# Grouped attention: probabilities as fp16 halves turned by the DMA engines, where TensorE turned them in fp32

## The chip, the cores and the metric

One core of a Trainium2 chip runs the whole program. The metric is the time of one execution on the device in microseconds; the figure quoted is the median of several executions. The profile is of one such execution.

## What is computed

Two transformer layers over x of 4 batches x 256 tokens x 256 features, in this order: layer norm and an attention over a cache of 1601 keys plus 256 new ones; layer norm and a mixture of 32 experts; layer norm and the grouped cross attention that the change is about; layer norm and a ternary-weight network. Each result is added to x. The grouped attention is this:

```python
q = (hidden_states @ Wq).reshape(B, S, N_HEADS, HEAD_DIM)                # 4, 256, 16, 128
k = (encoder_hidden_states @ Wk).reshape(B, S_enc, N_KV_HEADS, HEAD_DIM) # 4, 1601, 4, 128
v = (encoder_hidden_states @ Wv).reshape(B, S_enc, N_KV_HEADS, HEAD_DIM)
q = rms_norm(q, q_norm_w)
k = rms_norm(k, k_norm_w)
k = jnp.repeat(k, groups, axis=2)                                        # groups = 4
v = jnp.repeat(v, groups, axis=2)
scores = jnp.einsum('bqhd,bkhd->bhqk', q, k) * scale
probs = jax.nn.softmax(scores, axis=-1)
out = jnp.einsum('bhqk,bkhd->bqhd', probs, v)
out = out.reshape(B, S, N_HEADS * HEAD_DIM)
return out @ Wo
```

## The kernel before

The program is written as four stages by hand, each with one instruction stream per engine and semaphores between them: `cached_attention`, `experts`, `grouped_attention` and `bit_ffn`. Products keep nearly fp32 accuracy by splitting each operand in two: HI is the value rounded to the format of the multiplier (fp32r), LO the remainder, and `product` issues three matmuls, HI x HI, HI x LO and LO x HI (`PARTS`).

`grouped_attention` works in **groups**: one batch with one of the four key-and-value heads, 16 groups in all. A group has eight **steps**, one for each of its four query heads and each half of 128 tokens; N = 128 steps, and `DRAIN` = 4 more at the end. Two steps make a **unit**: one head of 256 tokens. In step n:

- PE computes the scores of 128 tokens against 1601 keys into four PSUM banks `ps_s`, twelve matmuls (line 2021).
- DVE takes the maximum over the keys in `largest` (lines 1987, 1989) and announces it negated (line 1992).
- ACT takes the exponentials into `probs` in two pieces, 1200 and 401 keys, with their sums (`exp`, line 1844).
- For an earlier unit, PE turns the probabilities in 13 tiles of 128x128 (line 2070) into the ring of three PSUM banks `ps_t`; ACT copies HI out of it (line 1836) and DVE makes LO (line 1971) into `pT`. These are the jobs "pT".
- PE weighs the values of the unit before that: `weigh`, 39 matmuls in two halves, into `ps_m`. ACT takes the result out (`take_values`, line 1852).
- The sums' inverses (`invert`, DVE lines 1998 and 2001) go once per unit as a row through DRAM and back to all partitions (`invert_rows`, SP); POOL multiplies the result with them (line 1735), ACT makes HI (line 1859) and POOL makes LO (line 1738) of `oT`.

Beside this, each step has small jobs for the next group, dealt out by the table in `prepared`: the queries (`q`), keys and values (`kv`, 7 jobs of two key tiles, DVE lines 1958, 1959, 1961), their normalisation (`q_eps`, `k_eps`; POOL lines 1715, 1719, 1725, 1728), their transposes (`qT`, `kT`, DVE line 1967), the weights' splits (`split_q`, `split_kv`, `split_out` on ACT and POOL), and the output projection of the group before (`y`). At a batch's start there are also `norm`, `xT` and the encoder's splits (`enc`). All of PE, ACT and DVE go through the same list `plan[n]` in order, and all ring jobs share the three banks in order: a job waits until the job three places before it has been emptied by DVE.

The values `v` and `pT` are fp32r pairs. In `experts`, beside the products of the experts, the first group's keys and values are prepared.

## Time and profile before

| | |
|---|---|
| median of 3 executions | 1645.3 us (1642.59 to 1646.03) |
| the profiled execution, its own time | 1644.8 us |
| its span, first to last instruction | 1642.7 us |
| mean granted TensorE clock | 0.955 |
| first attention, to the start of the routing | about 180 us |
| routing and experts | about 180 to 423 us |
| grouped attention, prologue | about 423 to 458 us |
| grouped attention, 128 steps and drain | 458 to 1569 us |
| ternary network | 1569 to 1643 us |
| DMA traffic | 128 MB, 83691 packets |

Times in the trace are microseconds from the span's first instruction. A busy engine is not yet the bound: what matters in a stage is for whom the others wait. PE stands for the matmuls and PEld for the loads of their stationary operand, which overlap; DVE is VectorE, ACT ScalarE, POOL GpSimd, and SP the queue that issues the DMAs.

### The profile page before, as it was taken

What the parts mean: (1) busy time and instruction counts of PE and PEld (TensorE: products, weight loads), DVE (VectorE), ACT (ScalarE), POOL (GpSimd) and SP (SyncE); (2) the same over time, 40 slices, a digit from 0 to 9 for tenths busy, and PEclk for the clock granted to TensorE, in tenths of its full rate; (3) what the DMA queues carried; (4) which work ended last, traced back from release to release, by engine and by line L of the source; (5) the groups of instructions that cost most, each with busy time, mean ns of one, the idle gap of its engine ahead of it and who ended that gap; (6) DMA issues with size and microseconds to landing.
All of it is one profiled execution on the core that took longest, in us unless ns stands there. A gap on an engine that the chain in (4) does not pass through costs nothing. (4 is left out here: it accounts for less than half of the span.)

```text
span 1642.7 us, 27599 instructions
## 1 busy us (share of the span) xinstructions
PE 1443.0 (88%) x10080; PEld 1347.7 (82%) x10080; DVE 1161.6 (71%) x2372; ACT 982.1 (60%) x2065; POOL 570.5 (35%) x477
## 2 busy tenths in 40 slices
PE   6998378887679899999999899999989999999945
PEld 5888268776569898899999899999989999999823
DVE  4765688887567776667777667776766777677657
ACT  4564177887356565665656566566656656656536
POOL 3342154443355232342323343332234323322135
PEclk9999589999799999999999999999999999999968
DMA  6241479998223020101102011010101101001010
GB/s 202 77 168 58 153 246 295 299 299 282 61 46 78 20 70 10 50 20 27 43 8 70 20 40 42 8 43 16 59 20 39 43 8 43 21 7 27 23 52 26
DMA packets 83691, 128.05 MB, mean 78 GB/s; under 512 B 17284, under 2 KB 63496, under 8 KB 83176
## 3 DMA queue, kind: packets, MB, share of 16 engines
q1 hardware_dynamic: 79000, 113.84, 21.8%
q0 software_dynamic: 4560, 12.46, 3.1%
q8 instruction: 83, 1.36, 0.4%
q14 instruction: 48, 0.39, 0.1%
HBM read 114.28 MB, written 11.99 MB: 77 GB/s over the span
## 5 line engine op out<-in xcount | busy, mean ns | idle before, releaser
L1836 ACT ACTIVATE ga_pT<-ga_ps_t 128x512 fp32r<-128x512 f32 (+1 forms) x512 | 243.9, 516 | 256.5 <-PE ga_ps_t L2070 255.7
L1971 DVE TENSOR_TENSOR ga_pT<-ga_ps_t,ga_pT 128x512 fp32r<-128x512 f32 (+1 forms) x512 | 280.3, 583 | 94.3 <-ACT ga_pT L1836 92.3
L1844 ACT ACTIVATE ga_probs<-ga_ps_s,ga_neg_max 128x1200 f32<-128x1200 f32 (+1 forms) x256 | 235.7, 927 | 90.0 <-DVE ga_neg_max L1992 89.7
L2070 PE MATMUL ga_ps_t<-all_eye,ga_probs 128*128 128x128 f32 (+1 forms) x1664 | 227.0, 274 | 9.7 <-DVE ga_pT L1971 9.6
L2070 PEld LDWEIGHTS ga_ps_t<-all_eye,ga_probs 128*128 128x128 f32 (+1 forms) x1664 | 192.8, 141 | 19.7 <-DVE ga_pT L1971 12.6
L1987 DVE TENSOR_REDUCE ga_part_max<-ga_ps_s 128x1 f32<-128x1200 f32 x128 | 178.8, 1397 | 12.0 <-PE ga_ps_s L2021 10.5
L1738 POOL TENSOR_TENSOR ga_oT<-ga_out_n,ga_oT 128x256 fp32r<-128x256 f32 x64 | 47.6, 744 | 394.9 <-ACT ga_oT L1859 394.9
L2021 PE MATMUL ga_ps_t<-side_w_kv,side_encT 128*128 128x256 f32 (+1 forms) x1170 | 164.4, 290 | 13.9 <-DVE ga_pT L1971 8.6
L2021 PE MATMUL ga_ps_m<-ga_pT,ga_v 128*128 128x256 f32 (+1 forms) x1248 | 174.0, 286 | 2.6 <-DVE ga_pT L1971 2.4
L2021 PE MATMUL ga_ps_m<-ga_pT,side_v 128*128 128x256 f32 (+1 forms) x1248 | 174.6, 287 | 0.6 <-DVE ga_pT L1971 0.5
L2021 PEld LDWEIGHTS ga_ps_t<-side_w_kv,side_encT 128*128 128x128 f32 (+1 forms) x1170 | 147.0, 188 | 23.5 <-DVE ga_pT L1971 11.4
L2021 PE MATMUL ga_ps_s<-side_kT,ga_qT 128*128 128x400 f32 (+1 forms) x768 | 157.5, 354 | 6.1 <-ACT ga_probs L1844 6.0
L2021 PEld LDWEIGHTS ga_ps_m<-ga_pT,ga_v 128*128 128x128 f32 (+1 forms) x1248 | 157.1, 189 | 5.8 <-DVE ga_pT L1971 4.3
L2021 PEld LDWEIGHTS ga_ps_m<-ga_pT,side_v 128*128 128x128 f32 (+1 forms) x1248 | 157.8, 190 | 2.8 <-DVE ga_pT L1971 1.4
L2021 PE MATMUL ga_ps_s<-ga_kT,ga_qT 128*128 128x400 f32 (+1 forms) x768 | 158.8, 357 | 0.0
L2021 PEld LDWEIGHTS ga_ps_s<-side_kT,ga_qT 128*128 128x128 f32 x768 | 139.3, 192 | 7.1 <-ACT ga_probs L1844 7.0
L2021 PEld LDWEIGHTS ga_ps_s<-ga_kT,ga_qT 128*128 128x128 f32 x768 | 140.7, 195 | 0.6 <-ACT ga_probs L1844 0.4
L1232 DVE TENSOR_TENSOR ex_w<-ex_raw,ex_w 128x1408 fp32r<-128x1408 f32 x63 | 106.3, 1687 | 28.5 <-ACT ex_w L1129 27.7
L1290 PE MATMUL ex_ps_g<-ex_w,ex_xT 128*128 128x448 f32 x378 | 93.8, 384 | 34.4 <-issue 24.0
L1725 POOL TENSOR_TENSOR side_k_scale<-side_k_sq_eps,all_half_power 128x8 f32<-128x8 f32 (+1 forms) x30 | 42.1, 1405 | 215.3 <-DVE side_k_sq_eps L1937 215.2
L1078 POOL DMA_INDIRECT ex_xg<-all_xn_rows,ex_token_u x63 | 76.4, 1213 | 112.0 <-PE ex_ps_x L1348 90.7
L1290 PEld LDWEIGHTS ex_ps_g<-ex_w,ex_xT 128*128 128x128 f32 x378 | 67.7, 192 | 49.0 <-issue 25.5
(274 smaller groups left out, 2617.4 us busy)
## 6 DMA issues: line engine op xcount, KB each, us to landing
ex_raw<-in_L_ffn_packed SPq DMA_DIRECT2D x63, 704.0 KB
side_w_q_raw<-in_L_xattn_Wq SPq DMA_DIRECT2D x16, 512.0 KB
side_w_q_raw<-in_L_xattn_Wo SPq DMA_DIRECT2D x16, 512.0 KB, 4.6
ga_inv_rows<-ga_inv_row SPq DMA_DIRECT2D x64, 128.0 KB, 3.1
mix_y_rows<-ex_y SPq DMA_DIRECT2D x63, 128.0 KB
side_enc<-in_ctx_turned SPq DMA_DIRECT2D x12, 512.0 KB, 5.3
ca_keys<-in_ctx_turned SPq DMA_DIRECT2D x12, 464.0 KB, 6.1
ca_cache<-in_ctx SPq DMA_DIRECT2D x4, 1024.0 KB, 8.3
```

The lines of the kernel that those rows point to most:

```text
L1078: nc.gpsimd.indirect_dma_start(xg[j % XGS][:, :], None, xn_rows[:, :], bass.IndirectOffsetOnAxis(ap=token_u[:, j:j + 1], axis=0)).then_inc ...
L1232: nc.vector.tensor_tensor(w[j % WS][:, LO, :], raw[j % RAWS][:, :], f32(w[j % WS][:, HI, :]), ALU.subtract).then_inc(w_lo, 1)
L1290: mm = nc.tensor.matmul(out, lhs(s), rhs(c), start=first and n == 0, stop=last and n == 2)
L1725: nc.gpsimd.tensor_tensor(k_scale[:, a:z], k_sq_eps[:, a:z], half_power[:, 0:z - a], ALU.pow).then_inc(k_scaled, 1)
L1738: nc.gpsimd.tensor_tensor(oT[:, LO, u % HG, :], out_n[:, :], f32(oT[:, HI, u % HG, :]), ALU.subtract).then_inc(out_lo, 1)
L1836: nc.scalar.activation(dst(HI), src, ACT.Copy, scale=scale).then_inc(read, 1)
L1844: nc.scalar.activation(dst, src, ACT.Exp, bias=neg_max[:, n % 2:n % 2 + 1], accum_out=half_sum[:, n % 4, k:k + 1]).then_inc(exped, 1)
L1971: nc.vector.tensor_tensor(dst(LO), src, f32(dst(HI)), ALU.subtract).then_inc(empty, 1)
L1987: nc.vector.tensor_reduce(part_max[:, 0:1], ps_s[:, 0:NB - 1, 0:WIDE], AX.XY, ALU.max)
L2021: mm = nc.tensor.matmul(out, lhs(a), rhs(c), start=first and n == 0, stop=last and n == 2)
L2070: mm = nc.tensor.transpose(out[0:top, i * P:(i + 1) * P], probs[step % PB][:, tile * P:tile * P + top], eye[:, :])
```

## The change

- In `grouped_attention` the jobs "pT" go. Each step's probabilities are made final at once: DVE computes the inverse of the step's row sum (`invert(n)`, now per step, times 2^15), ACT writes HI = fp16(probs x inverse) in two pieces of 1024 and 577 keys (`probs_high`), and DVE writes LO = fp16(probs x inverse - HI) in the same two pieces (`probs_low`). Both go to `halves`, two buffers. SP then issues two transposing DMAs per step (`turn_probs`), one for each half, 128 x 1664 fp16 to `pT`, now two buffers of fp16.
- DVE's order within a step changes: maximum, the jobs of the step before, inverse, low halves; in a group's first step the jobs come ahead of the maximum.
- ACT's order: both pieces of exp, the high halves, the result of `take_values` or `split_result`, then the ring jobs.
- The values are fp16 halves too, scaled by a power that keeps them in range: `experts` computes a bound for the largest value from the largest sum of squares of a cache row (twelve squares added to ACT in `cached_attention`) and the largest sum of squares of a column of Wv (two matmuls, a transposition, one more matmul, some small DVE instructions, one power on POOL). The 512 KB of Wv are loaded once more for it. `take_values` multiplies by `out_scale`.
- The row's round trip through DRAM, POOL's multiplication with it, and `PB`'s third buffer go.
- The small jobs are dealt anew; `norm` and `xT` of a new batch come six and five steps earlier relative to its group, into a buffer of their own (`xn_of`); `y` moves from steps 4 and 5 to 6 and 7, with `oT` in six places instead of four; `split_out` moves from step 7 to step 2 of the next group. `weigh` has 21 and 18 matmuls in its two halves instead of 24 and 15.

```diff
+            def turn_probs(n, part, ready):
+                u, t = n // QT, n % QT
+                sp.wait_ge(ready, 2 * n + 2)
+                if u >= 2:
+                    sp.wait_ge(out_ready, u - 1)
+                sp.dma_start(pT[u % 2][:, part, :, t * P:(t + 1) * P], halves[n % 2][:, part, :], transpose=True
+                             ).then_inc(turned[n % TURNS], 16)
...
             def exp(n, k):
                 if k == 0:
                     act.wait_ge(neg_ready, n + 1)
+                    if n >= PB:
+                        act.wait_ge(low, 2 * (n - PB) + 2)
...
+            def probs_high(n):
+                act.wait_ge(inverted, n + 1)
+                if n >= 2:
+                    act.wait_ge(*turned_through(n - 2))
+                for a, z in ((0, SPLIT), (SPLIT, KV)):
+                    nc.scalar.activation(halves[n % 2][:, HI, a:z], probs[n % PB][:, a:z], ACT.Copy,
+                                         scale=inv_sum[:, n % 2:n % 2 + 1]).then_inc(high, 1)
...
+            def invert(n):
+                dve.wait_ge(exped, 2 * n + 2)
+                nc.vector.tensor_scalar(row_sum[:, n % 2:n % 2 + 1], half_sum[:, n % 4, 0:1], half_sum[:, n % 4, 1:2],
+                                        1.0 / PROBS_TOP, ALU.add, ALU.mult).then_inc(summed, 1)
+                dve.wait_ge(summed, n + 1)
+                nc.vector.reciprocal(inv_sum[:, n % 2:n % 2 + 1], row_sum[:, n % 2:n % 2 + 1]).then_inc(inverted, 1)
+
+            def probs_low(n):
+                if n >= 2:
+                    dve.wait_ge(*turned_through(n - 2))
+                for k, (a, z) in enumerate(((0, SPLIT), (SPLIT, KV))):
+                    dve.wait_ge(high, 2 * n + k + 1)
+                    nc.vector.scalar_tensor_tensor(halves[n % 2][:, LO, a:z], probs[n % PB][:, a:z],
+                                                   inv_sum[:, n % 2:n % 2 + 1], halves[n % 2][:, HI, a:z],
+                                                   ALU.mult, ALU.subtract).then_inc(low, 1)
...
-            for n in range(N + DRAIN):
-                if n % 2 == 0 and 0 <= n // 2 - 1 < UNITS:
-                    invert(n // 2 - 1)
-                if n < N:
-                    largest(n)
-                for e in plan[n]:
-                    entry(e)
+            for n in range(N + DRAIN + 1):
+                first_of_group = n % STEPS == 0
+                if n < N and not first_of_group:
+                    largest(n)
+                if n:
+                    for e in plan[n - 1]:
+                        entry(e)
+                if n < N and first_of_group:
+                    largest(n)
+                if n < N:
+                    invert(n)
+                    probs_low(n)
...
             def weigh(half, piece, u):
                 if piece == 0:
-                    pe.wait_ge(*emptied(("pT", (QT - 1, 2 * half + 1), u)))
-                    if half == 0 and u:
-                        pe.wait_ge(u_here, u)
+                    if half == 0:
+                        for t in range(QT):
+                            pe.wait_ge(*turned_through(QT * u + t))
+                        if u:
+                            pe.wait_ge(u_here, u)
...
+                nc.scalar.activation(v[:, HI, at, :], cache[:, at, :], ACT.Square,
+                                     accum_out=routing.enc_squares[:, 3 * b + h:3 * b + h + 1]).then_inc(squared, 1)
+                act.wait_ge(squared, 3 * b + h + 1)
                 nc.scalar.activation(v[:, HI, at, :], cache[:, at, :], ACT.Copy).then_inc(v_hi, 1)
```

DVE in a step whose small job is a query projection, before (`ga_part_max` and `ga_neg_max` are the maximum, `ga_pT` the turned probabilities of an older unit, `ga_qn` and `ga_q_sq` the query job):

```order
L1987 TENSOR_REDUCE ga_part_max<-ga_ps_s 128x1
L1989 TENSOR_REDUCE ga_part_max<-ga_ps_s 128x1
L1992 TENSOR_REDUCE ga_neg_max<-ga_part_max 128x1
L1971 TENSOR_TENSOR ga_pT<-ga_ps_t,ga_pT 128x4x128
L1971 TENSOR_TENSOR ga_pT<-ga_ps_t,ga_pT 65x128
L1950 COPY ga_qn<-ga_ps_t 128x512
L1951 TENSOR_REDUCE ga_q_sq<-ga_squares_of 128x4
L1971 TENSOR_TENSOR ga_pT<-ga_ps_t,ga_pT 128x4x128
L1971 TENSOR_TENSOR ga_pT<-ga_ps_t,ga_pT 65x128
L1930 TENSOR_SCALAR ga_q_sq_eps<-ga_q_sq 128x8
L1998 TENSOR_TENSOR ga_row_sum<-ga_half_sum 128x2
L2001 RECIPROCAL ga_inv_sum<-ga_row_sum 128x2
```

and the same kind of step in the changed kernel, up to the next step's first maximum (`ga_halves` are the fp16 halves):

```order
L2046 TENSOR_REDUCE ga_part_max<-ga_ps_s 128x1
L2048 TENSOR_REDUCE ga_part_max<-ga_ps_s 128x1
L2051 TENSOR_REDUCE ga_neg_max<-ga_part_max 128x1
L2009 COPY ga_qn<-ga_ps_t 128x512
L2010 TENSOR_REDUCE ga_q_sq<-ga_squares_of 128x4
L1987 TENSOR_SCALAR ga_q_sq_eps<-ga_q_sq 128x8
L2056 TENSOR_SCALAR ga_row_sum<-ga_half_sum 128x1
L2059 RECIPROCAL ga_inv_sum<-ga_row_sum 128x1
L2066 SCALAR_TENSOR_TENSOR ga_halves<-ga_probs,ga_inv_sum,ga_halves 128x1024
L2066 SCALAR_TENSOR_TENSOR ga_halves<-ga_probs,ga_inv_sum,ga_halves 128x577
L2046 TENSOR_REDUCE ga_part_max<-ga_ps_s 128x1
```

The four copies of turned probabilities are gone from DVE; the inverse and the two low halves of the same step's probabilities stand ahead of the next maximum.

DVE at the end of a group in the changed kernel, from step 7's inverse to step 0's low halves:

```order
L2056 TENSOR_SCALAR ga_row_sum<-ga_half_sum 128x1
L2059 RECIPROCAL ga_inv_sum<-ga_row_sum 128x1
L2066 SCALAR_TENSOR_TENSOR ga_halves<-ga_probs,ga_inv_sum,ga_halves 128x1024
L2066 SCALAR_TENSOR_TENSOR ga_halves<-ga_probs,ga_inv_sum,ga_halves 128x577
L2004 TENSOR_TENSOR all_x<-all_x,ga_ps_t 128x256
L2026 SCALAR_TENSOR_TENSOR ga_kT<-ga_ps_t,side_qk_w,ga_kT 128x512
L2026 SCALAR_TENSOR_TENSOR ga_kT<-ga_ps_t,side_qk_w,ga_kT 128x65
L2046 TENSOR_REDUCE ga_part_max<-ga_ps_s 128x1
L2048 TENSOR_REDUCE ga_part_max<-ga_ps_s 128x1
L2051 TENSOR_REDUCE ga_neg_max<-ga_part_max 128x1
L2056 TENSOR_SCALAR ga_row_sum<-ga_half_sum 128x1
```

The last key copies (`ga_kT`) and `y` (into `all_x`) now stand between step 7's low halves and step 0's maximum; the next group's scores read these keys.

PE at a group's edge, before, from the last transposes of step 7 to the middle of step 0 and on:

```order
L2063 MATMUL ga_ps_t<-all_eye,side_kn 128x65
L2021 MATMUL ga_ps_s<-side_kT,ga_qT 128x400 x9
L2021 MATMUL ga_ps_s<-side_kT,ga_qT 128x402 x3
L2070 MATMUL ga_ps_t<-all_eye,ga_probs 128x128 x8
L2021 MATMUL ga_ps_m<-ga_pT,ga_v 128x256 x9
L2021 MATMUL ga_ps_t<-ga_w_in,ga_hT 128x512 x6
L2021 MATMUL ga_ps_m<-ga_pT,ga_v 128x256 x6
L2070 MATMUL ga_ps_t<-all_eye,ga_probs 128x128 x8
```

and now:

```order
L2135 MATMUL ga_ps_t<-all_eye,side_kn 128x128 x4
L2135 MATMUL ga_ps_t<-all_eye,side_kn 128x65
L2093 MATMUL ga_ps_s<-side_kT,ga_qT 128x400 x9
L2093 MATMUL ga_ps_s<-side_kT,ga_qT 128x402 x3
L2093 MATMUL ga_ps_m<-ga_pT,ga_v 128x256 x18
L2093 MATMUL ga_ps_t<-ga_w_in,ga_hT 128x512 x6
L2093 MATMUL ga_ps_s<-side_kT,ga_qT 128x400 x9
```

The transposes of `ga_probs` no longer stand around the scores; between the last `side_kn` transposition and the scores that read it PE has nothing else to issue.

## Rows read from the trace of the kernel before

**Rows 1.** The page's head: busy us, share of the span, instructions.

```profile
PE 1443.0 (88%) x10080; PEld 1347.7 (82%) x10080; DVE 1161.6 (71%) x2372; ACT 982.1 (60%) x2065; POOL 570.5 (35%) x477
```

**Rows 2.** DVE announcing a maximum: summary (ns min/median/max; first, last start), then timeline.

```profile
L1992 DVE TENSOR_REDUCE ga_neg_max<-ga_part_max x128: 154/155/158, 460.1 to 1545.6; 128x1 f32<-128x2 f32 x128
1083.91 0.15 DVE L1992 TENSOR_REDUCE ga_neg_max<-ga_part_max 128x1 f32<-128x2 f32 x1
1152.24 0.16 DVE L1992 TENSOR_REDUCE ga_neg_max<-ga_part_max 128x1 f32<-128x2 f32 x1
1227.74 0.16 DVE L1992 TENSOR_REDUCE ga_neg_max<-ga_part_max 128x1 f32<-128x2 f32 x1
```

**Rows 3.** Windows: length, busy us (count) by engine, PEclk, DMA share, GB/s.

```profile
460.30:515.60 55.30, 48.55 (x314) 45.76 (x315) 39.73 (x76) 33.60 (x70) 28.56 (x25) 0.94 0.26 59
590.40:1500.90 910.50, 873.70 (x6396) 838.34 (x6396) 641.32 (x1325) 567.90 (x1277) 298.60 (x236) 0.99 0.11 32
1500.90:1568.90 68.00, 61.46 (x459) 59.67 (x457) 39.10 (x74) 37.25 (x85) 13.49 (x14) 0.97 0.08 19
```

**Rows 4.** The page's costliest groups: busy us, mean ns, idle before.

```profile
L2070 PE MATMUL ga_ps_t<-all_eye,ga_probs 128*128 128x128 f32 (+1 forms) x1664 | 227.0, 274 | 9.7 <-DVE ga_pT L1971 9.6
```

**Rows 5.** Timeline of one step's maximum and exponentials: start us, us.

```profile
580.82 1.40 DVE L1987 TENSOR_REDUCE ga_part_max<-ga_ps_s 128x1 f32<-128x1200 f32 x1
582.73 0.15 DVE L1992 TENSOR_REDUCE ga_neg_max<-ga_part_max 128x1 f32<-128x2 f32 x1
582.92 1.26 ACT L1844 ACTIVATE ga_probs<-ga_ps_s,ga_neg_max 128x1200 f32<-128x1200 f32 x1 [0.44 <-DVE ga_neg_max L1992]
584.65 0.20 ACT L1844 ACTIVATION_READ_ACCUMULATOR ga_probs<-ga_ps_s,ga_neg_max 128x1 f32 x1
```

**Rows 6.** Groups by form, and timeline of one key-and-value job.

```profile
L1796 ACT ACTIVATE ga_w_in<-side_w_q_raw 128x1024 fp32r<-128x1024 f32 x16 | 17.1, 1067 | 0.8 <-PEq L904 0.8
L2005 DVE TENSOR_TENSOR ga_w_in<-side_w_q_raw,ga_w_in 128x1024 fp32r<-128x1024 f32 x1 | 1.2, 1225 | 3.4 <-ACT ga_w_in L1796 3.4
L1967 DVE SCALAR_TENSOR_TENSOR ga_kT<-ga_ps_t,side_qk_w,ga_kT 128x512 fp32r<-128x512 f32 x24 | 17.9, 748 | 22.4 <-ACT ga_kT L1836 22.4
555.97 0.43 DVE L1958 COPY side_kn<-ga_ps_t 128x256 f32<-128x256 f32 x1 [0.18 <-ACT ga_squares_of L1831]
556.64 0.41 DVE L1961 TENSOR_REDUCE side_k_sq<-ga_squares_of 128x2 f32<-128x256 f32 x1
```

**Rows 7.** Timeline of a DVE instruction beside POOL's; summary of DVE's row sum.

```profile
450.85 1.90 POOL L1719 TENSOR_TENSOR ga_qn<-ga_qn,ga_q_scale 128x1024 f32<-128x1024 f32 x1
451.27 1.50 DVE L1937 TENSOR_SCALAR side_k_sq_eps<-side_k_sq 128x5 f32<-128x5 f32 x1
L1998 DVE TENSOR_TENSOR ga_row_sum<-ga_half_sum x64: 147/154/527, 469.5 to 1549.1; 128x2 f32<-128x2 f32 x64
```

**Rows 8.** Groups of POOL in this stage.

```profile
L1738 POOL TENSOR_TENSOR ga_oT<-ga_out_n,ga_oT 128x256 fp32r<-128x256 f32 x64 | 47.6, 744 | 394.9 <-ACT ga_oT L1859 394.9
L1728 POOL TENSOR_TENSOR side_kn<-side_kn,side_k_scale 128x1024 f32<-128x1024 f32 (+1 forms) x30 | 47.4, 1579 | 2.4
```

**Rows 9.** Windows at a batch start.

```profile
652.00:659.00 7.00, 3.05 (x23) 2.44 (x22) 4.34 (x8) 2.99 (x7) 1.52 (x3) 1.00 0.34 96
659.00:666.00 7.00, 6.41 (x23) 6.07 (x24) 4.55 (x9) 2.88 (x8) 3.70 (x3) 0.51 0.01 1
```

**Rows 10.** Windows: first attention, and the routing ahead of the experts.

```profile
0.00:180.00 180.00, 144.30 (x950) 134.35 (x950) 109.26 (x221) 84.43 (x131) 55.30 (x45) 0.94 0.35 118
180.00:207.00 27.00, 9.35 (x44) 4.76 (x44) 17.68 (x58) 4.99 (x8) 8.05 (x16) 0.50 0.69 224
```

**Rows 11.** The page on DMA: rate in 40 slices, main queue, one load.

```profile
GB/s 202 77 168 58 153 246 295 299 299 282 61 46 78 20 70 10 50 20 27 43 8 70 20 40 42 8 43 16 59 20 39 43 8 43 21 7 27 23 52 26
q1 hardware_dynamic: 79000, 113.84, 21.8%
side_enc<-in_ctx_turned SPq DMA_DIRECT2D x12, 512.0 KB, 5.3
```

More of the change, by code:

```diff
@@ L22 @@
 LN_EPS = 1e-5
+VALUE_TOP = 2.0 ** 15
+PROBS_TOP = 2.0 ** 15
 class Signal:
@@ L1411, in grouped_attention @@
     key_tiles = side.key_tiles
-    pieces = [[range(0, 4), range(4, 8)], [range(8, 11), range(11, KT)]]
+    pieces = [[range(0, 4), range(4, 7)], [range(7, 10), range(10, KT)]]
     DRAIN = 4
@@ L1454, in prepared @@
+        if 0 < g < GROUPS and s in (6, 7):
+            jobs = [("y", s - 6, g - 1)] + jobs
         row, at = divmod(g + 2, G)
         if at == 0 and row < B:
-            late = late + {6: [("norm", 0, row)], 7: [("xT", 0, row)]}.get(s, [])
+            if s == 0:
+                jobs = jobs + [("norm", 0, row)]
+            if s == 2:
+                jobs = [("xT", 0, row)] + jobs
         row, at = divmod(g + 1, G)
         if at == 0 and row < B and s < 4:
-            late = late + [("enc", (0, 1, 3, 2)[s], row)]
+            jobs = jobs + [("enc", (0, 1, 3, 2)[s], row)]
@@ L1473, in grouped_attention @@
+        assert sum(e[0] in RING for e in jobs) <= TB
+        return ([("scores", 0, n)] if n < N else []) + weighed(n) + jobs
+    RING = ("xT", "q", "kv", "qT", "kT", "y")
     prologue = ([("kv", 0, 1), ("kv", 1, 1), ("kv", 2, 1), ("combine", 0, 0), ("kv", 3, 1), ("combine", 1, 0),
@@ L1500, in grouped_attention @@
             pass
-        pT = sb("pT", [P, 2, KT, S], F32R)
-        oT = sb("oT", [P, 2, HG, S], F32R)
+        pT = [sb(f"pT{i}", [P, 2, KT, S], F16) for i in range(2)]
+        oT = sb("oT", [P, QT + HG, 2, S], F32R)
+        halves = [sb(f"halves{i}", [P, 2, PADDED], F16) for i in range(2)]
         w_raw = side.w_q_raw
@@ L1566, in grouped_attention @@
         inverted = sem("inverted")
-        inv_out = sem("inv_out")
-        inv_in = sem("inv_in")
+        high = sem("high")
+        low = sem("low")
+        turned = [sem(f"turned{i}") for i in range(TURNS)]
         out_ready = sem("out_ready")
         u_here = sem("u_here")
-        out_here = sem("out_here")
         out_hi = sem("out_hi")
@@ L1654, in _ @@
                 g, s = n // STEPS, n % STEPS
-                u = (n - 2) // 2
-                if n % 2 == 0 and 0 <= u < UNITS:
-                    invert_rows(u)
+                if n < N:
+                    turn_probs(n, HI, high)
+                    turn_probs(n, LO, low)
                 if s == 1 and 0 < g and g + 2 < GROUPS:
@@ L1685, in _ @@
             nc.gpsimd.memset(f32(kT[1][:, :, KV:COLS_EVEN]), 0.0).then_inc(cleared, 1)
+            for part in (HI, LO):
+                for i in range(2):
+                    nc.gpsimd.memset(halves[i][:, part, KV:PADDED], 0.0).then_inc(cleared, 1)
             def split_q(g):
@@ L1887, in _ @@
                     split_result((n - 5) // 2)
+                for e in plan[n]:
+                    if e[0] == "enc":
+                        split_encoder(e[1], e[2])
+                    elif e[0] in RING and e[0] != "y":
+                        ring(e)
                 if n == 0:
```

269 lines of the change are left out of this document (136 added, 133 removed).

## The prediction

> **What bounds the kernel now.** I read the page's head first: PE 88% busy, DVE 71% [rows 1]. Shares over the whole run mix stages, so I next cut the grouped attention by the time at which DVE announces a step's maximum. It announces 128 of them, from 460.1 to 1545.6 us [rows 2]: two thirds of the run are 128 steps, eight to a group. Inside, groups 2 to 14 last 910.5 us, in which PE is busy for 873.7 (96%) and DVE for 641 [rows 3]. An ordinary group takes 68.3 us, and the one in which a new batch starts takes 75.5 [rows 2]; (910.5 - 3 x 75.5) / 10 gives 68.4 again. So the stage is bound by PE, at full clock (0.99), and a step of 8.5 us is what PE needs: scores, transposes of the probabilities, weighing, and the next group's projections.
>
> The change takes from PE its 1664 transposes of probabilities, 227 us [rows 4]: 1.8 us of each step. If PE stayed the bound, the stage would fall by over 200 us. It does not stay the bound. What matters is who follows, and that is read from the chain of one step.
>
> **The new chain.** In the order of the changed kernel (both DVE excerpts above), DVE does in step n: maximum(n), the small jobs of step n-1, the inverse of the row sum, the two low halves; only then comes maximum(n+1). Before, DVE's copies of turned probabilities belonged to an older unit, so nothing in a step waited for that step's own exponentials. Now DVE waits for ACT twice inside each step: for exp, then for the high half. By the rows:
> - maximum, from 580.82 to 582.88 [rows 5]: 2.06 us
> - hand-over 0.04; exp on ACT, 582.92 to 584.85 [rows 5]: 1.93
> - row sum and reciprocal, two small instructions at 0.15 (the minimum of the present row sum [rows 7]) plus three hand-overs: 0.40
> - high half of 1024 columns on ACT: 1.07, as the copy of 1024 [rows 6]; hand-overs 0.07. The other 577 run beside the low half.
> - low halves on DVE. A 1024-column subtraction of two SBUF tensors takes 1.23, a scalar_tensor_tensor of 512 takes 0.75 against PSUM [rows 6]; I take 1.25 + 0.81 - 0.1 of overlap = 1.95.
> Sum 7.5 us. The jobs lie beside exp as long as they are shorter than 2.0 us. Two key-and-value jobs are 2.1 us (1.08 each, from 555.97 to 557.05 [rows 6]), so two steps have 7.6, the one with a small eps instruction as well 7.8, the one with qT 7.7, and three stay at 7.5. Step 0 of a group is different: its maximum needs the new keys' scores, which need the last kT copies, and DVE makes those only after the low halves of step 7 (second DVE excerpt, and PE's). It costs 7.5 + 1.3 (y and kT on DVE) + 1.9 (nine score matmuls with the hand-over) = 10.7. A group: 3 x 7.5 + 2 x 7.6 + 7.8 + 7.7 + 10.7 = 63.9 us. PE's work in a step after the change is 8.5 - 1.8 = 6.7 us on average, so it waits for 10 to 15% of the time; the two-job steps come close to 7.7 and may add 0.3. So 64.2.
>
> **What comes on top.** (1) The low halves read two SBUF tensors. DVE's instructions on small SBUF operands stand still while POOL works: one of 128x5 took 1.50 us, from 451.27 to 452.77, and ended with POOL's multiplication (450.85 + 1.90 = 452.75); the present row sum takes between 0.147 and 0.527 [rows 7]. DVE's large instructions in this stage read PSUM and are untouched today (0.75 for each kT copy). This is the row that I weigh highest. POOL has in a group two normalisations of keys (1.58 on average), one of queries (1.90), their powers, weight splits, and four low parts of results (0.74 each) [rows 7, 8]. By position: the query normalisation starts 3.5 us into a step and runs over the row sum and the start of the low half (1.6 us lost), the two key normalisations cost 0.2 and 0.8, the four low parts and the splits together 1.4. That is 4.0 us a group. Bounds: 0 if DVE always comes first; 9 if POOL also slips in between the two low instructions. (2) At each group's edge PE now sits idle for about 4.5 us. In 652 to 659 us it was busy for 3.05 of 7 us, and for the 7 us that follow the clock was 0.51, so 1.2 GHz [rows 9]; twelve score matmuls then need twice as long. I take 1 us a group, bounds 0 and 4. So 64.2 + 4.0 + 1.0 = 69.2 us, where 68.3 stand now: +0.9 for 13 groups, **+12 us**.
>
> The Trainium skill (SBUF — State Buffer, section "SBUF: two separate sides") makes this a rule: DVE with two SBUF inputs and a GpSimd instruction that reads SBUF share one port pair, held for a whole instruction. The trace agrees, by the 1.50 us above. By a reading without it the group would be 65.2 and the term -40.
>
> **The rest, by parts.**
> - Batch starts: the norm moves from step 6 to step 0 and its transposition from 7 to 2, each into a buffer of its own, so most of the 7.2 us extra goes; the encoder splits stay. I take 3 us saved at each of three: -9 (bounds -22 and 0).
> - Group 0 has few jobs and takes 55.3 us [rows 3]; eight chain steps are 60, with POOL's share 62: +7. In the last group seven steps took 1545.6 - 1500.9 = 44.7 [rows 2, 3]; seven chain steps are 52.5: +8. These two are the clearest losses: there PE's work was short, the chain is not. The drain after the last maximum (23 us now) exchanges transposes and the inverse's round trip for one DMA transposition: 0.
> - Twelve squares of the cache on ACT in the first attention, 1.07 or more each [rows 6]: 13 us of work on an engine that is busy for 84 of the first 180 us [rows 10]; bounds 0 and 13, taken 3.
> - The bound for the values: 27 us before the experts in which PE is busy for 9.4 [rows 10], a chain. To it come two matmuls, some ten small DVE instructions, one power on POOL and a 512 KB load. They partly run while POOL gathers rows: taken 4, bounds 0 and 9.
> - fp16 values and probabilities: same number of matmuls, 256 columns each; cover is PE's new slack, so 0.
> - Inverse rows: 64 round trips through DRAM and POOL's 64 multiplications go; nobody waited long for them, and POOL's part is counted in (1).
> Sum: 12 - 9 + 7 + 8 + 3 + 4 = +25; POOL's freed multiplications should take about 5 off the collisions: **+20**. The profiled execution took 1644.8 us (span 1642.7 and 2.1 around it), 0.5 under the median of 1645.3. Forecast **1665 us**, slightly slower. Its own range, with the bounds of the collisions and of the clock, is 1640 to 1725.
>
> **Rival A, faster: no collisions.** If the low halves are always issued first, and the clock holds, a group is 64.2 and the 13 groups save 53: 1645 - 53 - 9 + 15 + 7 = 1605 us. For it: DVE issues the second low half before the first has ended, so the port may never be free in between. Against: 1.50 us in rows 7. A measurement of this kernel can tell some 0.2% (3 us) from no change. Chance 0.31.
>
> **Rival B, slower: the DMA queue sets the pace.** Each step has two transpositions of 128 x 1664 fp16, 426 KB each, on SP's queue, one after the other; PE needs the second some 6 us after the low half is done, and both must fit in one step. The trace has none. Lower bound: 426 KB at 299 GB/s (the best stretch [rows 11]) is 1.4 us. Upper: 79000 packets took 21.8% of 16 engines' 1642.7 us, 73 ns each [rows 11]; if a transposition is 128 x 13 pieces of 256 bytes, each engine has 104, 7.5 us. The mean packet there is 1441 bytes, so the upper end is for far larger pieces, and I take 3 us; a plain 512 KB load lands in 5.3 us [rows 11], most of which overlaps. At 3 us the pair takes 6 and hides. It decides from about 4.3 us each. At 5 us a step is 10, and 127 steps take 1270 instead of 1085: 1645 + 185 + 7 = 1837 us. At 7.5 it would be near 2470. Chance 0.17.
>
> The Trainium skill (DMA: Bandwidth & Descriptors, section "Latency and other measured facts") gives 261 GB/s for a transposition, an estimate of 1.6 us here, by which this rival would fall; no run here shows it yet.
>
> **Rival C: no change.** The losses at both ends and the gains in the middle cancel within 0.2%: 1642 to 1648. It needs collisions near 3 us a group, inside my bounds. Chance 0.07.
>
> **How the numbers follow.** The forecast has 0.45, A 0.31, B 0.17, C 0.07. A's side gives faster 0.31 plus the 0.03 of the forecast's range that lies below: 0.34. Same 0.07. Slower: 0.42 + 0.17 = 0.59. The range takes in A's time and half of B: 1600 to 1800.
>
> **What would show it.** Groups 2 to 14 at about 69 us between equal steps; PE's share there down to 80 to 85% with DVE waiting for ACT's probabilities twice a step; low halves of 1.25 us with a tail up to 3 us, each long one ending with a POOL instruction; a half-clock stretch after group edges; a first maximum to last maximum of about 1100 us. Wrong if the low halves are all alike in length (A), or if PE or ACT waits for the transpositions in every step (B).

## The result, and the profile after

The change made the kernel slower: **1726.7 us** (median, 1723.9 to 1730.0, 4 runs) against 1643.9 us of the kernel before beside it (1639.1 to 1646.0, 4 runs), a ratio of 1.051 with a 95% interval from 1.048 to 1.054. I had forecast 1665. The direction was right, and the time lay in the wide range of 1600 to 1800, which takes in the rivals. But the loss was four times the forecast (+82.8 us, forecast +20), and the time lay just outside the forecast's own range of 1640 to 1725.

The page's head after the change, and its first DMA queue (to compare with [rows 1] and [rows 11]):

```profile
PE 1315.6 (76%) x8423; PEld 1151.6 (67%) x8423; DVE 1265.1 (73%) x2252; ACT 1004.1 (58%) x1834; POOL 557.8 (32%) x419
q1 hardware_dynamic: 495016, 214.99, 54.2%
```

PE fell from 88% to 76% busy, and no other engine rose to where PE had been. When the most used engine is at 76% and the kernel is slower, the time is in waiting. Next the same view as [rows 2], DVE announcing a maximum: the summary, then the starts of groups 8 to 12 (group 0 is the first).

```profile
L2051 DVE TENSOR_REDUCE ga_neg_max<-ga_part_max x128: 154/155/156, 464.3 to 1618.8; 128x1 f32<-128x2 f32 x128
1055.66 0.15 DVE L2051 TENSOR_REDUCE ga_neg_max<-ga_part_max 128x1 f32<-128x2 f32 x1
1126.53 0.15 DVE L2051 TENSOR_REDUCE ga_neg_max<-ga_part_max 128x1 f32<-128x2 f32 x1
1197.71 0.15 DVE L2051 TENSOR_REDUCE ga_neg_max<-ga_part_max 128x1 f32<-128x2 f32 x1
1270.94 0.15 DVE L2051 TENSOR_REDUCE ga_neg_max<-ga_part_max 128x1 f32<-128x2 f32 x1
1352.29 0.15 DVE L2051 TENSOR_REDUCE ga_neg_max<-ga_part_max 128x1 f32<-128x2 f32 x1
```

Groups 8 and 9 take 70.9 and 71.2 us, where an ordinary one took 68.3. Group 10, which holds the norm, takes 73.2; before it took 75.5 [rows 2]. Group 11, which holds the encoder's splits, takes 81.35; before it took 67.8 (its neighbour in the trace before starts at 1295.56). So the extra of a batch start moved to another group and grew. The windows of [rows 3] after the change (groups 2 to 14; group 11; the last group's seven steps):

```profile
604.34:1563.51 959.17, 764.52 (x5045) 676.03 (x5044) 727.53 (x1221) 570.77 (x1066) 287.46 (x182) 0.92 0.59 115
1270.94:1352.29 81.35, 57.77 (x382) 51.25 (x380) 57.10 (x93) 46.41 (x85) 29.00 (x17) 0.91 0.54 107
1563.51:1618.94 55.43, 41.04 (x246) 35.38 (x245) 31.97 (x51) 29.52 (x50) 5.11 (x4) 0.86 0.58 106
```

Groups 2 to 14 grew by 959.2 - 910.5 = 48.7 us. The rest of the 79.2 by which the spans differ: 4.2 ahead of the first maximum, 9.6 in group 0 (65.0 for 55.4), 0.3 in group 1, 10.5 in the last group's seven steps, 6.0 behind the last maximum.

Next the low pairs, the two low halves that DVE makes in each step. Three kinds of long ones stand out. Start, us, engine, of three consecutive steps of group 2, with POOL's row where it matters; an ordinary group has the same three (group 5 at 849.72, 858.69 and 867.14):

```profile
625.45 1.90 POOL L1774 TENSOR_TENSOR ga_qn<-ga_qn,ga_q_scale 128x1024 f32<-128x1024 f32 x1
625.88 3.28 DVE L2066 SCALAR_TENSOR_TENSOR ga_halves<-ga_probs,ga_inv_sum,ga_halves 128x1024 f16<-128x1024 f32 x2 [1.28 <-ACT ga_halves L1906]
635.44 2.50 DVE L2066 SCALAR_TENSOR_TENSOR ga_halves<-ga_probs,ga_inv_sum,ga_halves 128x1024 f16<-128x1024 f32 x2 [1.29 <-ACT ga_halves L1906]
636.39 0.93 POOL L1789 TENSOR_TENSOR ga_oT<-ga_out_n,ga_oT 128x256 fp32r<-128x256 f32 x1 [4.45 <-ACT ga_oT L1922]
643.90 3.66 DVE L2066 SCALAR_TENSOR_TENSOR ga_halves<-ga_probs,ga_inv_sum,ga_halves 128x1024 f16<-128x1024 f32 x2 [1.29 <-ACT ga_halves L1906]
644.09 2.85 POOL L1783 TENSOR_TENSOR side_kn<-side_kn,side_k_scale 128x1024 f32<-128x1024 f32 x1
```

A pair with no POOL instruction near it takes 2.02 us (468.06, 475.69 and others in group 0). These take 3.28, 2.50 and 3.66. In the first, POOL's multiplication is under way when the pair starts and ends at 625.45 + 1.90 = 627.35; the pair is 1.26 us longer than alone, as if DVE stood still until near that end. In the other two POOL begins while DVE's first piece runs, is itself held (0.93 and 2.85, where the same instructions take 0.74 and 1.90 alone), runs between the two pieces and holds the second. A fourth, 3.95 us, stands beside the split of the query weights. Four pairs of 2.49 and the three of 3.28, 3.66 and 3.95 are longer than 2.02 by (4 x 0.47) + 1.26 + 1.64 + 1.93 = 6.7 us a group.

And group 11, where PE waits:

```profile
1303.58 1.07 ACT L1859 ACTIVATE side_encT<-side_enc 128x1024 fp32r<-128x1024 f32 x1
1308.49 1.64 POOL L1780 TENSOR_TENSOR side_k_scale<-side_k_sq_eps,all_half_power 128x8 f32<-128x8 f32 x1 [5.06 <-DVE side_k_sq_eps L1994]
1310.20 2.85 POOL L1783 TENSOR_TENSOR side_kn<-side_kn,side_k_scale 128x1024 f32<-128x1024 f32 x1
1313.01 2.68 POOL L1755 TENSOR_TENSOR side_encT<-side_enc,side_encT 128x1024 fp32r<-128x1024 f32 x1
1315.84 4.86 PE L2093 MATMUL ga_ps_t<-side_w_kv,side_encT 128*128 128x256 f32 x24 [11.35 <-POOL side_encT L1755]
```

The releaser that PE's row names is POOL's encoder split, but that is only the last link. Its input was there at 1304.65. POOL stood 5.06 us in front of the key normalisation, which is ahead in its order and whose input DVE makes a step later, and only then came to the encoder. The new dealing puts both into step 3 and has PE use the piece in step 4; before, they stood apart.

### The profile page after: what moved, and what is told of

It reads as the page before. It is cut to its first block and busy times, and to the rows that moved or that the text cites. A ratio compares the mean times of both kernels' runs of the same rounds, so it can differ in the third digit from the quotient of the medians.

```text
span 1721.9 us, 24069 instructions
## 1 busy us (share of the span) xinstructions
PE 1315.6 (76%) x8423; PEld 1151.6 (67%) x8423; DVE 1265.1 (73%) x2252; ACT 1004.1 (58%) x1834; POOL 557.8 (32%) x419
## 3 DMA queue, kind: packets, MB, share of 16 engines
q1 hardware_dynamic: 495016, 214.99, 54.2%
## 5 line engine op out<-in xcount | busy, mean ns | idle before, releaser
L2066 DVE SCALAR_TENSOR_TENSOR ga_halves<-ga_probs,ga_inv_sum,ga_halves 128x1024 f16<-128x1024 f32 (+1 forms) x256 | 356.5, 1433 | 164.8 <-ACT ga_halves L1906 164.8
L1906 ACT ACTIVATE ga_halves<-ga_probs,ga_inv_sum 128x1024 f16<-128x1024 f32 (+1 forms) x256 | 233.2, 958 | 83.2 <-DVE ga_inv_sum L2059 81.7
L2093 PE MATMUL ga_ps_s<-side_kT,ga_qT 128*128 128x400 f32 (+1 forms) x768 | 176.9, 384 | 45.8 <-DVE side_kT L2026 24.4
L2093 PE MATMUL ga_ps_m<-ga_pT,ga_v 128*128 128x256 f16 (+1 forms) x1248 | 161.4, 289 | 18.4 <-ACT ga_out_n L1914 11.6
L2093 PE MATMUL ga_ps_m<-ga_pT,side_v 128*128 128x256 f16 (+1 forms) x1248 | 155.5, 282 | 9.2 <-ACT ga_out_n L1914 8.5
L2093 PEld LDWEIGHTS ga_ps_m<-ga_pT,ga_v 128*128 128x128 f16 (+1 forms) x1248 | 124.4, 104 | 51.3 <-issue 32.0
L2093 PEld LDWEIGHTS ga_ps_m<-ga_pT,side_v 128*128 128x128 f16 (+1 forms) x1248 | 121.2, 101 | 40.1 <-issue 23.6
L2093 PE MATMUL ga_ps_t<-ga_w_out,ga_oT 128*128 128x256 f32 x384 | 63.5, 324 | 48.4 <-DVE all_x L2004 23.6
L2093 PEld LDWEIGHTS ga_ps_t<-ga_w_out,ga_oT 128*128 128x128 f32 x384 | 56.3, 222 | 56.5 <-DVE all_x L2004 27.5
L1157 ACT ACTIVATE ex_w<-ex_raw 128x1408 fp32r<-128x1408 f32 x63 | 87.5, 1389 | 2.8 <-DMA ex_raw<-in_L_ffn_packed 2.7
```

The lines of the kernel that those rows point to most:

```text
L1157: nc.scalar.activation(w[j % WS][:, HI, :], raw[j % RAWS][:, :], ACT.Copy).then_inc(w_hi, 1)
L1906: nc.scalar.activation(halves[n % 2][:, HI, a:z], probs[n % PB][:, a:z], ACT.Copy, scale=inv_sum[:, n % 2:n % 2 + 1]).then_inc(high, 1)
L2066: nc.vector.scalar_tensor_tensor(halves[n % 2][:, LO, a:z], probs[n % PB][:, a:z], inv_sum[:, n % 2:n % 2 + 1], halves[n % 2][:, HI, a:z], ...
L2093: mm = nc.tensor.matmul(out, lhs(a), rhs(c), start=first and n == 0, stop=last and n == 2)
```

## The experiments

Theory 1: three separate losses, (a) the chain of one step, maximum to low half, 7.7 us, as in the prediction; (b) POOL beside the low pair, 6.7 us a group; (c) POOL's order at a batch start, 10 us. Rivals: the transpositions' queue (e8), the dealing's load of work itself (e9 keeps the dealing), and PE's clock, which no run sets by itself.

### e1: the low half a step later

DVE makes the low halves of step n-1 behind the maximum of step n.

```diff
+                if 1 <= n <= N:
+                    probs_low(n - 1)
+                if n < N and not first_of_group:
+                    invert(n)
                 if n:
                     for e in plan[n - 1]:
                         entry(e)
                 if n < N and first_of_group:
                     largest(n)
-                if n < N:
                     invert(n)
-                    probs_low(n)
...
-        u, half = ((n - 3) // 2, 0) if n % 2 else (n // 2 - 2, 1)
+        u, half = ((n - 5) // 2, 1) if n % 2 else (n // 2 - 2, 0)
```

> DVE makes the low halves of step n-1 behind the maximum of step n (beside the exponentials), the inverse of step n after them; weighing, the result's copies and the drain come one step later. Theory 1 (the chain maximum, exponential, inverse, high half, low half of one step sets the time of a step): the high half and the low pair (1.15 + 2.0 to 2.5 us) leave the chain, DVE's own work (maximum 2.1, low pair 2.5, inverse 0.4, jobs 1.7 on average, so 6.7 us) and PE's 6.7 us become the bound; an ordinary group falls from 71.1 to 57-62 us, and the whole from 1727 to 1560-1610 us, below the kernel before. Rival (the transpositions' latency, or the clock that falls at group edges, sets the step): the group stays at 69-72 us and the whole at 1700-1735.

Measured: 1716.1 us (ratio 1.046, 1.043 to 1.048). The rival's number, but not by its reason. The groups stayed at 71 to 73 us, with the time elsewhere in them. The first two steps of a group fell from 7.7 and 8.2 to 5.9 and 5.6 us, below all that the chain allowed; the steps with two key-and-value jobs rose to between 8 and 14. From the timeline of one of them:

```profile
772.83 4.25 DVE L2067 SCALAR_TENSOR_TENSOR ga_halves<-ga_probs,ga_inv_sum,ga_halves 128x1024 f16<-128x1024 f32 x2
777.32 0.41 DVE L2018 COPY side_kn<-ga_ps_t 128x256 f32<-128x256 f32 x1
778.17 2.93 PE L2096 MATMUL ga_ps_t<-side_w_kv,side_encT 128*128 128x256 f32 x12 [3.43 <-DVE ga_v L2019]
780.89 3.84 PE L2096 MATMUL ga_ps_s<-side_kT,ga_qT 128*128 128x400 f32 x12
784.13 1.41 DVE L2047 TENSOR_REDUCE ga_part_max<-ga_ps_s 128x1 f32<-128x1200 f32 x1 [4.65 <-PE ga_ps_s L2096]
```

The low pair (4.25 us in this step, where POOL works beside it as well) now runs ahead of the copies that empty PE's three banks; PE waits 3.43 us for a bank, the scores are queued behind that product, and DVE waits 4.65 us for the scores. The chain was cut and a circle between PE and DVE took its place. My expectation priced DVE's work and not where its jobs stand. What it leaves open is whether the order of the jobs is all that is missing: e7.

### e2: POOL waits for the low halves

```diff
+            def after_low(n):
+                if n >= STEPS:
+                    pool.wait_ge(low, min(2 * (n + 2), 2 * N))
...
             def query_norm(g, n=0):
...
                 pool.wait_ge(q_scaled, g + 1)
+                after_low(n)
...
                 pool.wait_ge(out_hi, u + 1)
+                pool.wait_ge(low, min(2 * (2 * u + 6), 2 * N))
```

The same line stands in the key normalisation and the three weight splits.

> POOL's large instructions (query and key multiplications, the three weight splits, the low part of each result) wait until the low halves of the step are done, so that none runs beside them; nothing is left out. Theory 1 (POOL beside the low halves stretches them: pairs of 2.49, 3.28, 3.66 and 3.95 us against 2.02 alone, 6.7 us in an ordinary group, all of it on the chain): all pairs at 2.0 us, ordinary groups 71.1 -> 64.5-66, whole 1727 -> about 1640. Rival (the stretch is not POOL's, or POOL's delayed products hold PE instead): pairs unchanged, or as much new waiting of PE for POOL; whole 1715-1735.

Measured: 1643.7 us (10 runs; ratio 1.0015, 1.0001 to 1.0028). Added waits took 83 us off, and brought the changed kernel level with the one before. Low halves by form, of the change and of e2 (busy, mean ns, idle before):

```profile
L2066 DVE SCALAR_TENSOR_TENSOR ga_halves<-ga_probs,ga_inv_sum,ga_halves 128x1024 f16<-128x1024 f32 x128 | 207.6, 1622 | 164.8 <-ACT ga_halves L1906 164.8
L2066 DVE SCALAR_TENSOR_TENSOR ga_halves<-ga_probs,ga_inv_sum,ga_halves 128x577 f16<-128x577 f32 x128 | 159.3, 1244 | 0.0
```

```profile
L2076 DVE SCALAR_TENSOR_TENSOR ga_halves<-ga_probs,ga_inv_sum,ga_halves 128x1024 f16<-128x1024 f32 x128 | 165.0, 1289 | 164.9 <-ACT ga_halves L1916 162.3 <-issue 2.6
L2076 DVE SCALAR_TENSOR_TENSOR ga_halves<-ga_probs,ga_inv_sum,ga_halves 128x577 f16<-128x577 f32 x128 | 104.6, 817 | 0.0
```

The pair fell from 1.62 + 1.24 to 1.29 + 0.82, 97 us in 128 steps. POOL's own multiplications are back at 1.90 as well. Ordinary groups take 63.9 to 64.5 us, and the chain sum of the prediction was 64.2. Batch starts still took 77 to 79: POOL, which now waits, came later to the encoder's splits, and PE waited for them twice at each batch start, 2.8 and 9.9 us.

### e3: the encoder's splits two steps earlier

```diff
-        row, at = divmod(g + 1, G)
-        if at == 0 and row < B and s < 4:
-            jobs = jobs + [("enc", (0, 1, 3, 2)[s], row)]
+        row, at = divmod(n + 2 + STEPS, G * STEPS)
+        if at < 4 and 0 < row < B:
+            jobs = jobs + [("enc", (0, 1, 3, 2)[at], row)]
...
-                    if at == (G - 1) * STEPS + 1:
+                    if at == (G - 1) * STEPS - 1:
```

> The four encoder splits of a new batch are dealt two steps earlier (steps 6, 7, 0, 1 instead of 0, 1, 2, 3), and the load of the last piece with them. Theory 1 (the 10 us by which a batch start is longer than an ordinary group is PE's wait for the encoder's low part): batch-start groups 81.1 -> 72-74, whole 1727 -> 1700-1706. Rival (the extra lies in POOL beside DVE and in the half clock behind it, wherever the splits stand): batch-start groups 79-81, or their time found in the group ahead; whole 1720-1730.

Measured: 1707.5 us (ratio 1.040, 1.037 to 1.043). Batch-start groups took 72.7, 72.6 and 73.3 us; norm groups rose by 1.5 to 2. A gain of 19 us where theory 1 had 21 to 27. PE no longer waits for the encoder anywhere in the stage; what is left over an ordinary group is one step of 10.9 us where an ordinary group has 9.0, and in the norm groups one of 11.6 instead of 9.7. Both vanish in e5, where POOL waits, so POOL's work beside the low pairs is the likely cause.

### e4: POOL's instructions made short

```diff
+                z = WQ if g == 1 else 8
-                nc.gpsimd.tensor_tensor(w_in[:, LO, 0:WQ], w_raw[:, :], f32(w_in[:, HI, 0:WQ]),
+                nc.gpsimd.tensor_tensor(w_in[:, LO, 0:z], w_raw[:, 0:z], f32(w_in[:, HI, 0:z]),
```

The other instructions are cut alike. This kernel leaves out most of the low parts and of the two normalisations from the second group on, so it is not a kernel to use, only a measure of what POOL's work costs.

> From the second group on POOL's large instructions compute 8 columns (per tile or head) instead of all; the low parts of the query, key, output and encoder weights, of the results and the normalisation of queries and keys are so left out for the rest. Same order and waits. Theory 1: every low pair takes 2.0 us, ordinary groups 71.1 -> 64-65, batch starts 81 -> 66-70, whole about 1620-1640. Rival (the pairs' length is not POOL's doing): pairs stay at 2.5 to 3.9, ordinary groups above 70.

Measured: 1623.7 us (one run). Ordinary groups 63.9 to 64.8, batch starts 70.9 to 71.8. The ordinary group is no shorter than in e2: for DVE, a POOL that waits was as good as one with next to nothing to do. What e4 has over e2 lies in the batch starts.

### e5: e2 and e3 together

> e2 and e3 together: POOL waits for the low halves, and the encoder's splits come two steps earlier. If POOL's place beside the low halves and the encoder's place are two separate losses, they add: e2's batch-start groups (77-79 us) come down to 68-70, its norm groups rise by 1.6 as in e3 (73.4 -> 75.0), whole 1644 -> 1615-1622, below the kernel before. If POOL's later start now holds the encoder's splits back instead, nothing is gained over e2: 1638-1645.

Measured: **1602.3 us** (ratio 0.975, 0.973 to 0.977), below the kernel before. The two gains add to more than I expected: 83 + 19 would be 1624. So the losses are not quite separate. The batch starts have no extra left at all (64.5, 63.9, 63.9 us): the two waits for the encoder that e2 still had are gone (in group 11 POOL has the last piece done at 1216.5, and PE uses it at 1220.6), and so are the long steps that e3 still had.

### e6: only the results' low part waits

```diff
                 pool.wait_ge(out_hi, u + 1)
+                pool.wait_ge(low, min(2 * (2 * u + 6), 2 * N))
```

> Only the low part of a result (POOL, 0.93 us, four in a group) waits for the low halves; POOL's other work stays as in the change. Theory 1: the pairs of every second step fall from 2.49 to 2.02 us, four in a group, 1.9 us a group and 30 us in 16 groups: whole 1727 -> 1697. Rival (a small instruction of POOL costs only its own length where the chain has slack, so below half of it is seen): 1712-1727.

Measured: 1698.4 us (ratio 1.035, 1.033 to 1.037), 28 us less than the change. The 577-column piece fell from 1244 to 1016 ns on average, the 1024-column piece stayed at 1622. The low part of a result, 0.74 us of POOL's work, cost 28 us, as it stood beside the chain in every second step.

### e7: the low half later, the jobs first

e1 with the small jobs ahead of the low pair, and ACT's high halves behind the copies out of PE's three banks; the POOL waits of e2 (moved by a step; none at the splits) and the encoder of e3.

```diff
                 if n:
                     for e in plan[n - 1]:
                         entry(e)
                 if n < N and first_of_group:
                     largest(n)
+                if 1 <= n <= N:
+                    probs_low(n - 1)
                 if n < N:
                     invert(n)
-                    probs_low(n)
...
                     exp(n, 0)
                     exp(n, 1)
-                    probs_high(n)
...
                     elif e[0] in RING and e[0] != "y":
                         ring(e)
+                if n < N:
+                    probs_high(n)
```

> As e1 the low halves of step n-1 are made in step n, but behind the small jobs, so that PE's banks come free early; ACT makes the high halves behind the ring's copies; POOL's normalisations and results wait for the low halves; encoder two steps earlier. e1's steps with two key-and-value jobs took 9-14 us since PE waited for the banks that DVE emptied after the low pair. Theory 1a (e1 exchanged the chain for that wait, nothing else): no step above 8 us but the first of a group, ordinary groups 56-61, whole 1560-1595. Rival (with the chain gone PE's clock or DVE's own work holds the step near 8 us anyway): ordinary groups 63-70, whole 1610-1690.

Measured: **1455.8 us** (ratio 0.886, 0.884 to 0.888), 186 us below the kernel before. Ordinary groups take 54.2 to 54.6 us. Groups 2 to 14:

```profile
581.44:1313.15 731.71, 696.97 (x5046) 632.95 (x5044) 648.60 (x1221) 573.73 (x1066) 282.19 (x182) 0.99 0.80 151
```

PE is busy for 697 of 731.7 us, 95%, as it was before the change (96% [rows 3]), at the same clock of 0.99. The stage is back at PE's pace, with the transposes gone. DVE is at 89%. I had bounded PE's step by 6.7 us, 53.6 a group, and then widened the expectation of a group to 56 to 61; that was 1.6 us too careful. The expected whole, 1560 to 1595, was over 100 us too high for another reason: thirteen groups of 56 us are 728, close to the 731.7 measured, so the whole had not been added up from the groups. The norm groups (60.5 us) and batch starts (56.2 to 56.9) are still longer than an ordinary one; no run goes into that.

### e8: one more transposition in every second step

```diff
+                if part == LO and n % 2:
+                    sp.dma_start(spare[:, :, :], halves[n % 2][:, HI, :], transpose=True
+                                 ).then_inc(turned[n % TURNS], 16)
```

> The changed kernel with one more transposition of 128 x 1664 in every second step (the high halves once more, into a spare buffer, waited for like the others): 320 instead of 256. If the queue has slack, as the trace says (PE waited for it 7.5 us in all), the time stays within 5 us of 1727. If the queue's pace is near the bound (Rival B of the prediction), each of the 64 adds its own 1.5 to 4 us: 1820-1980.

Measured: 1728.0 us (ratio 1.053, 1.050 to 1.056), 1.3 us above the change and within its spread; groups 2 to 14 take 958.9 us, in the change 959.2. Rival B of the prediction falls.

### e9: the new order alone

e7 without POOL's waits and with the encoder where the change has it.

> e7 without the waits of POOL and with the encoder's splits where the change has them: the order of DVE, ACT and PE alone. If the low pair no longer stands on the chain that sets the step, POOL beside it costs little (in the change 6.7 us of an ordinary group): ordinary groups 54-56.5, batch starts 8-12 longer, whole 1480-1515. If DVE is still what PE waits for, the 6.7 us come back: ordinary groups 59-61, whole 1560-1590.

Measured: 1488.1 us (ratio 0.904, 0.901 to 0.908). Ordinary groups 54.7 to 55.1, batch starts 66.5 to 67.6. POOL beside the low pair, 6.7 us a group in the change, costs 0.5 once the pair is off the chain. The order of DVE, ACT and PE alone (with the results' low parts and the low transpositions moved along with it) is worth 239 of the 271 us between the change and e7. From e1 to e9 two things moved: DVE's small jobs went ahead of the low pair, and ACT's high halves behind the copies. No run has one without the other.

### e10: one square instead of twelve

```diff
+                if b == 0 and h == 0:
+                    nc.scalar.activation(v[:, HI, at, :], cache[:, at, :], ACT.Square,
+                                         accum_out=routing.enc_squares[:, 0:1]).then_inc(squared, 1)
```

> The changed kernel with one of the twelve squares of the cache in the first attention; the bound for the values then rests on that one part, the rest of its chain stays. In the two traces the last exponentials of the first attention are 5.5 us later after the change (161.9 against 156.4), the token lists 5.4 (203.3 against 197.9). If the squares make that, and the bound's chain after them costs nothing: whole 1727 -> 1721-1723, token lists at 198-199. If the later start is a spread of this stage between programs (it read 466 to 471 for the first maximum in other runs of the same head): no shift, 1724-1730.

Measured: 1721.5 us (ratio 1.048, 1.044 to 1.051), token lists at 198.8 us. The squares cost about 5 us: POOL's first gather by these lists starts at 199.9, and at 204.4 to 208.6 in the change and in every other experiment, which all keep the squares. The bound's chain behind them costs nothing that shows, but a few microseconds could hide: the first maximum comes at 458.8 us here and at 460.1 before the change, while kernels that are alike up to it spread from 464.3 to 471.4.

### e11: the encoder first in POOL's step

```diff
-                for e in plan[n]:
+                for e in sorted(plan[n], key=lambda e: e[0] != "enc"):
```

> In the change POOL's encoder split of step 3 stands behind the key normalisation, whose input DVE makes a step later (at a batch start: ACT's high part 1303.58, POOL's power 1308.49, multiplication to 1313.05, then the encoder's low part to 1315.7, PE held for 11.3 us). Here only POOL's order within a step is turned round, encoder first. If that order is the cause: the low part is done near 1307, PE's wait falls to 2-3 us, batch-start groups 81.1 -> 72-74, whole 1727 -> 1700-1706, as e3. If the late load or POOL's speed beside DVE makes the wait, batch starts stay above 78.

Measured: 1695.9 us (ratio 1.033, 1.031 to 1.035). Group 11 now takes 70.9 us instead of 81.35, no longer than an ordinary one. The rows of the same piece in this kernel's group 11:

```profile
1284.37 1.07 ACT L1859 ACTIVATE side_encT<-side_enc 128x1024 fp32r<-128x1024 f32 x1
1285.51 2.17 POOL L1755 TENSOR_TENSOR side_encT<-side_enc,side_encT 128x1024 fp32r<-128x1024 f32 x1 [1.29 <-ACT side_encT L1859]
1287.83 4.60 PE L2093 MATMUL ga_ps_t<-side_w_kv,side_encT 128*128 128x256 f32 x24 [2.57 <-POOL side_encT L1755]
1289.27 1.64 POOL L1780 TENSOR_TENSOR side_k_scale<-side_k_sq_eps,all_half_power 128x8 f32<-128x8 f32 x1 [1.59 <-DVE side_k_sq_eps L1994]
```

The wait is 2.57 us, not 11.35. At each of the three batch starts POOL's encoder split changed places with the key normalisation (step 3) and also with the query normalisation (step 1), and 31 us went. The wait that shrank is the one behind the key normalisation.

## Why the prediction came out as it did

**What bounds the kernel, and the new chain: right.** PE gave up the bound, and the chain maximum, exponential, inverse, high, low took it. The sum for a group on the chain alone was 64.2 us; e2 has 63.9 to 64.5. Its parts: low pair 1.95, measured 2.02; high half 1.07, measured 1.15; a plain step 7.5, in e2 7.7; the first step of a group 10.7, in e2 9.7 to 10.2. So two small errors cancel, and that the sum fits to 0.3 us is partly luck. PE's share of waiting, 10 to 15%, was also too low by its own numbers (6.7 us of work in a step of 8.0 leave 16%); in the change PE is busy for 80% of groups 2 to 14. Group 0 and the last group were forecast at +7 and +8 and came to +9.6 and +10.5, the short collisions with POOL in them included.

**The step that failed first: item (1) of "What comes on top", the collisions, 4.0 us a group.** The mechanism, POOL holding DVE's instructions on SBUF tensors, was the right one and the one that I said I weighed highest; the term was mis-sized. It measured 6.7 us: that much lies in the pairs of the change, and e2, which only keeps POOL away from them, takes an ordinary group from 71.1 to 64.2. The query multiplication I had at 1.6 (1.26 measured), the key normalisations at 0.2 and 0.8 (1.64 and 0), the four low parts and the splits at 1.4 together: 1.9 for the low parts alone and 1.93 for one split. I had placed them by the start of the low pair only. POOL also gets in between the two pieces, which I had put into the upper bound of 9, and with the results' low parts it did so four times a group. The "5 off" for POOL's freed multiplications was wrong outright: that work had not been in the 4.0, so nothing could come off. In 13 groups the two make 35 + 5 us.

The Trainium skill (SBUF — State Buffer, section "SBUF: two separate sides") has this as a lock that whoever starts first holds for a whole instruction. The traces agree: DVE's pair takes 3.28 us instead of 2.02 when POOL was first, and POOL's 0.74 becomes 0.93 when DVE was first. That a hold lasts for one instruction also leaves room for POOL between two of DVE's. The 1.50 us that the prediction set beside this rule belong to an instruction with one SBUF tensor as input; the case of two is shown by the pairs here.

**The step that failed second: batch starts, -9.** "The norm moves, most of the 7.2 us extra goes" held: the norm group fell from 75.5 to 73.2. "The encoder splits stay" was true of their step and false of what stands around them: the key normalisation moved from step 4 into step 3, ahead of them on POOL, and the fifth key job moved up to step 4. Measured 10 us at each of three; in e11, where only POOL's order differs, these groups are down at 70.9 to 71.4. With the norm groups the three batches cost 24 us more than forecast.

**The clock, 1.0 us a group: too much.** The clock did fall (0.92 in groups 2 to 14, 0.99 before), but 64.2 and 6.7 already make 70.9 of the 71.1 us of an ordinary group; with the chain as the bound PE had room for it. The errors partly cancel: +35 +5 +24 -13 = 51, against 50.7 missed in groups 2 to 14. Outside them the terms made 7 + 8 + 3 + 4 = 22 us, and 30.5 were measured.

**The smaller terms.** The squares were taken at 3 and cost 5 (e10); the value bound was taken at 4 and cost nothing that shows; together 7 against 4.2 up to the first maximum, a difference within the spread of this stage (e10). The drain was taken at 0. Behind the last maximum the program is 6.0 us longer. Of this 3.6 is the drain itself, by PE's timeline of the two kernels' ends:

```profile
1629.18 6.70 PE L2093 MATMUL ga_ps_m<-ga_pT,ga_v 128*128 128x256 f16 x39 [6.75 <-DMA ga_pT<-ga_halves]
1640.58 4.61 PE L2093 MATMUL ga_ps_t<-ga_w_out,ga_oT 128*128 128x256 f32 x24 [4.70 <-POOL ga_oT L1789]
```

With nothing left to do meanwhile, PE waits 6.75 us for the last transposition. It then works off 39 matmuls at a granted clock of 0.66. The other 2.4 us lie in the last layer, which the change doesn't touch. Its last sixteen matmuls take 3.36 us (from 1712.85, clock 0.64) where they took 2.11 (from 1634.93, clock 0.90); why the clock differs there, and the rest, stays open.

**The rivals.** A (no collisions): its group of 64.2 us is what e2 shows. Its whole of 1605 us is close to e5's 1602, but e5 also moves the encoder's splits, which A did not suppose; e2 without that has 1644, so the closeness is partly luck. A did not come about, since POOL is first at some pairs and gets in between the two pieces of others. B (the queue's pace) is out by e8 and by the trace: PE waited for transpositions 7.5 us in two places. In q1's rows, if all the packets that came on top are the transpositions', 416,016 packets took (0.542 x 1721.9 - 0.218 x 1642.7) x 16 / 256 = 36 us of one engine's time for each transposition, 2.2 us with all sixteen; I had taken 3, between 1.4 and 7.5. The Trainium skill (DMA: Bandwidth & Descriptors, section "Latency and other measured facts") gives 261 GB/s for a transposition, an estimate of 1.6 us: nearer than my value, and still 0.6 short here.

What I did not price at all is what e7 and e9 found: the same instructions in another order are worth 239 us (e9), and with POOL's waits and the encoder's place 271 (e7). The prediction named the two waits of DVE for ACT in each step, and took them as the price of the new scheme, when they were only the price of its order.

## What to carry to other kernels

When a change takes the busiest engine's work away, write down the longest chain inside one step of the loop before counting any engine's load. If a product is needed only two steps later, its making should not stand ahead of the next step's start; and where it is moved, the small copies that free another engine's buffers go in front of it (e1 against e9, which moved ACT's high halves too). Where an instruction on the chain read two SBUF tensors, the POOL instructions beside it were paid for by the chain: look for pairs of unequal length with a POOL row next to the long ones, and let POOL wait. And when jobs are dealt anew, read each in-order engine's queue for a job that stands behind another whose input comes later.

## What the runs showed that I had not expected

- POOL in a gap between two back-to-back DVE instructions: an instruction that takes 0.74 us alone costs DVE 0.47 us each time, 28 us in the program (e6). That happens although, with POOL away, the second piece starts before the first has ended (1.29 + 0.82 us make a pair of 2.02).
- A kernel got 83 us faster by added waits alone (e2).
- The same 5,045 matmuls of groups 2 to 14 were 764.5 us of PE's busy time in the change, at a granted clock of 0.92, and 697.0 in e7 at 0.99. PE waited for 20% of the time in the one and for 5% in the other, and had the lower clock where it waited more. While the chain sets the time this hardly shows. What the higher clock gave e7 no run separates.
- The DMA engines are 80% busy in e7's groups 2 to 14, most of it with transpositions (two a step at the 2.2 us worked out above), and PE waits for none there (its one wait, 6.5 us, is in the drain). By an estimate from these numbers, 0.80 x 6.8 us is 5.4 us of all engines' time a step; a step that short would have the DMA engines full.
